# Values of eight tiles projected ahead of the key combine in an attention and ternary feed-forward layer

## The reference

```
h = ln(x)
q = softmax((h Wq^T + bq) Wfq^T + bfq) over all 1024 features; k likewise with Wk, Wfk
v = h Wv^T + bv
per head (16 heads of 64): scores = q k^T; probs = scores / rowsum(scores); ctx = probs v
x = x + ctx
u = ln(x); x = x + bitlinear(silu(bitlinear(u, w_gate)) * bitlinear(u, w_up), w_down)
bitlinear: activations rounded to 127 steps of the row maximum, weights to -1, 0, 1 times their mean magnitude
```

## Time and profile before

| | |
|---|---|
| time, median of 3 runs | 1144.21 us (1143.06 to 1147.94) |
| the profiled execution's own time | 1148.11 us |
| its span on core 4, the slowest | 1146.6 us |
| spans of the other cores | 1123.3 to 1136.8 us |
| TensorE busy, core 4 | 1080.8 us (94%) |
| ScalarE, VectorE, GpSimd busy | 43%, 55%, 18% |
| moved by DMA | 199.66 MB, mean 174 GB/s |

### The profile page before, as it was taken

How to read it: one execution, slowest core, us unless ns; L and a number is a source line. 1 busy time by engine, 2 the same in 40 slices (tenths; PEclk the granted TensorE clock), 3 DMA queues, 4 the chain that set the end, 5 groups by cost and what they waited for, 6 DMA issues and landing times.

```text
span 1146.6 us, 13483 instructions; the slowest of 8 cores (1123.3 to 1146.6 us)
## 1 busy us (share of the span) xinstructions
PE 1080.8 (94%) x5379; PEld 503.7 (44%) x5414; DVE 632.1 (55%) x1140; ACT 491.1 (43%) x604; POOL 204.4 (18%) x132
## 2 busy tenths in 40 slices
PE   5859999999999999897879999999999999999998
PEld 2324454554444544342334444444444444444443
DVE  3356555667766667774826636645645645744311
ACT  2326776677787757564533123223223222222110
POOL 0000000023333330453322012012012012011010
PEclk9979899999998999998989999999999999999999
DMA  8969998689999977779971441441342351231240
GB/s 271 290 198 339 338 334 294 244 276 325 316 325 324 326 222 220 183 215 191 170 132 37 111 96 42 101 108 40 92 105 52 83 120 37 74 92 37 56 110 38
DMA packets 201263, 199.66 MB, mean 174 GB/s; under 512 B 170096, under 2 KB 170096, under 8 KB 193008
## 3 DMA queue, kind: packets, MB, share of 16 engines
q1 hardware_dynamic: 179392, 174.68, 54.2%
q10 hardware_dynamic: 21808, 24.12, 7.5%
HBM read 148.45 MB, written 29.36 MB: 155 GB/s over the span
## 4 chain that ended last, share of the span: by engine, by line
PE 79%; DMA 10%; DVE 4%; ACT 3%; POOL 2%; issue 1%; SPq 1%; ACTq 0%; DVEq 0%
PE ps L563 32%; PE ps L415 25%; PE ps L543 19%; DMA wst<-wdT 4%; DMA stage<-wfkT 2%; DMA wst<-wgT 2%; DMA bvb<-bv 2%; PE ps L464 1%; PE ps L453 1%; SPq L233 1%; ACT wd L348 1%; POOL hmid L1186 1%; POOL wst L326 1%; DVE hmid L1013 1%; DMA xr<-x_oth 1%
## 5 line engine op out<-in xcount | busy, mean ns | idle before, releaser
L563 PE MATMUL ps<-wg,aqT 128*128 128x512 fp8e4 x1024 | 244.9, 382 | 8.6 <-ACT silu L1136 6.0
L563 PE MATMUL ps<-wu,aqT 128*128 128x512 fp8e4 x1024 | 243.2, 381 | 4.1 <-DVE hmid L1013 4.1
L1136 ACT ACTIVATE silu<-ps,l 128x512 f32<-128x512 f32 x128 | 87.7, 686 | 319.5 <-PE ps L563 302.4
L1013 DVE SCALAR_TENSOR_TENSOR hmid<-ps,l,silu 128x512 f32<-128x512 f32 x128 | 95.7, 748 | 146.4 <-PE ps L563 102.2
L326 POOL TENSOR_SCALAR wst<-wst,msum 128x2048 f32<-128x2048 f32 x48 | 95.9, 2001 | 398.6 <-DMA wst<-wgT 292.5
L563 PEld LDWEIGHTS ps<-wu,aqT 128*128 128x128 bf16 x1024 | 100.2, 98 | 127.3 <-DVE hmid L1013 6.3
L563 PEld LDWEIGHTS ps<-wg,aqT 128*128 128x128 bf16 x1024 | 98.8, 99 | 122.4 <-ACT silu L1136 7.1
L415 PE MATMUL ps<-wck,xT 128*128 128x512 bf16 x509 | 127.8, 408 | 13.8 <-DVE xT L745 11.3
L1186 POOL TENSOR_SCALAR hmid<-hmid,hsc 128x1024 f32<-128x1024 f32 x64 | 70.4, 1118 | 306.2 <-DVE hsc L1034 306.2
L415 PE MATMUL ps<-wv,xT 128*128 128x512 bf16 x484 | 116.2, 392 | 5.7 <-ACT ek L1068 3.9
L1005 DVE SCALAR_TENSOR_TENSOR xr<-ps,hsc,xr 128x512 f32<-128x512 f32 x32 | 24.0, 751 | 168.3 <-PE ps L543 168.3
(11 more groups left out here) (95 smaller groups left out, 1064.6 us busy)
## 6 DMA issues: line engine op xcount, KB each, us to landing
wst<-wgT SPq DMA_DIRECT2D x32, 1024.0 KB, 10.6
wst<-wuT SPq DMA_DIRECT2D x32, 1024.0 KB, 9.0
wst<-wdT ACTq DMA_DIRECT2D x19, 1024.0 KB, 7.0
xr<-x_own SPq DMA_DIRECT2D x32, 512.0 KB, 6.9
s_hq<-hqs SPq DMA_DIRECT2D x32, 512.0 KB, 4.1
wst<-wdT SPq DMA_DIRECT2D x13, 1024.0 KB, 8.9
xr<-x_oth SPq DMA_DIRECT2D x16, 512.0 KB, 12.1
y<-xr SPq DMA_DIRECT2D x16, 512.0 KB, 3.4
```

Source lines behind the costliest of these rows:

```text
L563: pe(lambda e, c=c: e.matmul(out, a[:, c * 128:c * 128 + 128], w8[:, c * DI + 512 * oc:c * DI + 512 * oc + 512], start=(c == 0), stop=(c = ...
L1013: dv(lambda e: e.scalar_tensor_tensor(hmid[:, 512 * oc:512 * oc + 512], U[oc % 2], l2[:, s + 6:s + 7], sl, op0=ALU.mult, op1=ALU.mult), [a ...
L1136: ac(lambda e: e.activation(silu[:, (oc % 2) * 512:(oc % 2) * 512 + 512], G[oc % 2], ACTF.Silu, bias=0.0, scale=l2[:, s + 5:s + 6]), [at(" ...
```

## The change

Before slot 0, the values of tiles 0 to 7 come first and the key combine after them.

- Loads: x 0 and 1, then the wvT chunks among x 2 and 3, x 4 to 7, then wfkT in whole rows, then wk in eight blocks of 512 rows by 256 columns (1 KB pieces), bfk, then the first eight of wq and wfqT. bfq and bv come in slot 2. Each bias has its own semaphore, and `BKe` waits for bfk alone.
- TensorE: values of tiles 0 to 3 chunk by chunk in all eight banks (`pe_v4`, in an order sorted by written arrival times), after their transposes in the same banks (`pe_xt4`). Values of tiles 4 to 7 as items, each after the transposes of the next tile. Then eight items `CK` m, each a row block of wck, which waits for all of wfkT and the two wk blocks of column group m div 2; `BK`; `pe_k(0)`; `pe_k(1)`.
- The eight value tiles stay raw in f32 (`vraw`): four in the place of `wcq`, four in the first two `wst` buffers. `ac_ve` reads them there. Hence the query combine's copies wait for `VE`, `cq_slot` is one slot later (5 to 13), and the units of slots 3 to 7 alternate between the last two `wst` buffers (`NB` is 8).
- The units are spread by a nominal slot length (`slot_len`) over slots 3 to 29: 1, 1, 2, 2, 2 in slots 3 to 7, then 3, 4, 3, 3, 3, 3, 3, 2, then in slots 16 to 29 3, 3, 3, 4, 3, 3, 3, 3, 4, 3, 3, 2, 2, 3, and none in 30 and 31.
- `xT` has eight places at first, since tiles 0 to 7 wait there for their key items.

```diff
+    chunks += [rows("wvT", j, wv) for j in range(CH)]
+    chunks += [rows("wfkT", j, wfT) for j in range(CH)]
+    chunks += [block(b, h) for b in range(4) for h in range(2)]
     for j in range(CH):
-        chunks += [("wk", j, 0, D, wnat), ("wfkT", j, 0, 512, wfT)]
...
-        chunks += [("wq", j, 0, D, wnat), ("wfqT", j, 0, D, wfT)]
+        chunks += [rows("wq", j, wnat), rows("wfqT", j, wfT)]
...
     def on_dve(n):
-        return n % 2 == 0
+        return n >= 8 and (n % 2 == 0 if n < NV else n % 4 != 3)
...
+    def pe_v4(i, j):
+        for h in range(2):
+            pe(lambda e, h=h: e.matmul(
+                ps[:, 1024 * i + 512 * h:1024 * i + 512 * h + 512],
+                xT_of(i)[:, j * 128:j * 128 + 128],
+                wv[:, j * D + 512 * h:j * D + 512 * h + 512],
+                start=(j == 0), stop=(j == CH - 1)),
+               [at("XTe", i), cast_of("wvT", j)] if h == 0 else (),
+               ("V", i) if h == 1 and j == CH - 1 else None)
...
-    pe_xt(0)
+    pe_xt(4)
+    for i in range(4, NE):
+        if i + 1 < NE:
+            pe_xt(i + 1)
+        pe_v(i)
+    for m in range(CH):
+        item(("CK", m), lambda c, m=m: wnat[:, c * D + m * 128:
+                                            c * D + m * 128 + 128],
+             w_rhs(wfT), [cast_of("wfkT", 7), cast_of("wfkT", 6),
+                          cast_of("wk", 2 * (m // 2)),
+                          cast_of("wk", 2 * (m // 2) + 1)],
+             ("CK", m), at("CKe", m))
+    item("BK", brep_lhs(0), w_rhs(wfT), [at("brep", 0)], ("BK",), at("BKe"))
     pe_k(0)
-    pe_xt(1)
     pe_k(1)
     for i in range(TKV):
-        pe_v(i)
+        if i >= NE:
+            pe_v(i)
...
     for i in range(TKV):
-        if i < 4:
-            for n in range(NV + 4 * i, NV + 4 * i + 4):
+        if i < 2:
+            for n in range(NV + 8 + 4 * i, NV + 12 + 4 * i):
                 load_chunk(n)
-        if i + 4 < TKV:
+        if i == 2:
+            load_bias("bfq", bqc, ("bfq",))
+            load_bias("bv", bvb, ("biases",))
+        if 4 <= i < TKV - 4:
             load_x(i + 4)
...
+    def v_raw(i):
+        b = (ps[:, 1024 * i:1024 * i + 1024] if i < 4 else
+             AB[item_bank[("V", i)]])
+        evac("v" if i == 2 else "a", vraw(i), b, [at("V", i)], ("VR", i))
...
+    for i in range(5, NE):
+        dv_in(i)
+        dv_xte(i)
+        cast_chunk(2 * i - 2)
+        cast_chunk(2 * i - 1)
+        v_raw(i - 1)
```

More of the change, by code:

```diff
@@ L30 @@
 DEFER = 5
+NE = 8
 NWST = 4
@@ L301, in build_nc @@
     unit_id = {k: n for n, k in enumerate(units)}
-    wslot_of = [n % NWST if n < NA else (n - NA) % NWF
-                for n in range(len(units))]
+    cq_slot = {5 + m: m for m in range(9)}
+    slot_len = [4 + (4 if i >= NE else 0) +
+                (4 if i in cq_slot or TQ <= i < TKV - DEFER else 0)
+                for i in range(TKV - 2)]
+    slot_units = {i: [] for i in range(TKV)}
+    for n in range(NA):
+        want = sum(slot_len[:3]) + (n + 1) * sum(slot_len[3:]) / NA
+        slot_units[next(i for i in range(TKV - 2) if sum(
+            slot_len[:i + 1]) >= want - 1e-6)].append(n)
+    unit_slot = {n: i for i, l in slot_units.items() for n in l}
+    NB = len([n for n in range(NA) if unit_slot[n] < NE])
+    wslot_of = [2 + n % 2 if n < NB else (n - NB) % NWST if n < NA else
+                (n - NA) % NWF for n in range(len(units))]
     before = {}
@@ L306, in build_nc @@
         earlier = [m for m in range(n) if wslot_of[m] == s]
-        before[n] = at("unit", earlier[-1]) if earlier else None
+        before[n] = (at("unit", earlier[-1]) if earlier else
+                     at("VE", 2 * s + 5) if s < 2 else None)
     last_x = max(m for m in range(len(units)) if wslot_of[m] == NWST - 1)
@@ L417, in item @@
                     start=(c == 0), stop=(c == CH - 1)),
-                   (list(after) + [bank_free[b], also_free[b]])
+                   (list(after) + [bank_free[b]])
                    if h == 0 and c == 0 else (),
@@ L426, in x_lhs, with bank4, pe_xt4 @@
     def x_lhs(i):
[L427 to L442, removed]
+        x = xT_of(i)
+        return lambda c: x[:, c * 128:c * 128 + 128]
+    def bank4(i):
+        return ps[:, 1024 * i:1024 * i + 512].bitcast(BF16)
+    def pe_xt4(i):
+        for c in range(CH):
+            pe(lambda e, c=c: e.transpose(
+                bank4(i)[:, c * 128:(c + 1) * 128],
+                xh[:, c * 128:(c + 1) * 128], identb[...]),
+               [at("XH", i), at("ids")] if c == 0 else (),
+               ("XT", i) if c == CH - 1 else None)
+    def pe_v4(i, j):
[7 more added lines that the diff above has]
+               ("V", i) if h == 1 and j == CH - 1 else None)
+    x_in = [9.9, 12.9, 16.3, 21.1]
+    w_in_at = [9.8, 11.4, 14.6, 16.2, 19.4, 21.0, 22.6, 24.2]
+    order4 = [(x_in[i] - 1.4, i, -1) for i in range(4)]
+    order4 += [(max(x_in[i], w_in_at[j]), i, j) for i in range(4)
+               for j in range(CH)]
+    for _, i, j in sorted(order4):
+        if j < 0:
+            pe_xt4(i)
+        else:
+            pe_v4(i, j)
     def brep_lhs(k):
         return lambda c: brep[:, k * D + c * 128:k * D + c * 128 + 128]
-    item("BK", brep_lhs(0), w_rhs(wfT), [at("brep", 0)], ("BK",), at("BKe"))
-    t_free = [at("CKe", 4, 1)]
+    t_free = [at("VR", 2)]
     def pe_xt(i):
```

194 lines of the change are left out of this document (104 added, 90 removed).

## The result

The kernel became slower: 1183.12 us (median of 3 runs, 1182.06 to 1185.04) against 1144.21 of the kernel before in the same comparison. The ratio is 1.0335, with an interval of 1.0292 to 1.0377. The forecast was 1144, the range ended at 1153.

The account below looks back on a forecast made before the run. Phase 1 on core 4 bound by matmuls and 74 weight units, almost together; loads gain 8.3 us, the tail gives back 8.6: +0.3 on 1148.1, less 3.9, 1144.5, said as 1144. Own range 1137 to 1150; with rivals 1130 to 1153.

Parts of the forecast that it names:

- The early stage, step by step: Walk from the first loads through values and key combine to chunk 32, put at 95.3 us.
- pays for the late start: Phase 1 loads: old DMA room at 180 to 260, some 16 us, covers the 12 us late start and leaves 4.
- First matmul near 11: Start of the kernel: TensorE's first matmul was to come near 11 us.
- The last eight matmuls ... 26.6: Values of tiles 0 to 3: after the last wvT chunk's cast, eight matmuls of 1.7 us end them at 26.6.
- Tiles 4 to 7 then go at VectorE's pace ... 4.8: Values of tiles 4 to 7: a VectorE round of 4.8 us against 3.9 for TensorE, V 7 ending at 50.8.
- Combine to chunk 32: Before slot 0: combine starts at 54, eleven items take 38 us to 92, chunk 32 leaves at 95.3.
- Rival C: Early stage: half-clock matmuls make BK late, units go out at 103 instead of 95, time 1152; chance 0.18.
- Rival D: Early loads: x 5 to 7 wait for `xh` of tiles 1 to 3, making wfkT late; 1150 to 1155, chance 0.05.
- K-only slots: Slots 0 to 3, only a K each: 6.0 us a slot, `pe_kv(4)` at about 120.
- From 97 on ... 303: Phase 1 loads after 97: 45.1 and 54.3 MB at 337 and 322 GB/s, 303 us, last unit landing at 399.5.
- The tail: End of phase 1: from unit 73 to the last `pe_kv` 14.2 us, before 5.6, giving back 8.6.
- the 9% of the prediction's line: wk loads: 1 KB pieces 9% slower by a straight line through time per piece, 1.1 us on 4.2 MB, hidden by slack.

Follow-up runs that it names:

- ids_first: Changed kernel with the small identity that the first transposes wait for loaded second instead of tenth; 1173.58 us, ratio 1.0277.
- ids_r_ahead: ids_first plus the next tile's statistics and inverse deviation ordered ahead of the raw copy of the value item before; 1168.07 us, ratio 1.0208.
- gap_two: Changed kernel with units 0 and 1 and x 8 to 11 loaded ahead of chunk 32, the units' sums behind the combine's copies; 1167.3 us, ratio 1.0237.
- before_light: Kernel before with each of the 74 phase 1 units loading a quarter of its columns (other quantized weights and output); 1128.41 us, one run.
- units_to_31: Changed kernel with its units spread over slots 3 to 31 instead of 3 to 29; 1173.75 us, ratio 1.028.
- before_spread: Kernel before with only the changed kernel's number of units in each slot; 1147.14 us, ratio 1.005.
- best: Changed kernel with ids_r_ahead, units_to_31 and gap_two joined, and chunks 24 to 26 cast ahead of the first key logits; 1166.9 us, ratio 1.0199.
- all_four: Changed kernel with ids_r_ahead, units_to_31 and gap_filled joined; 1171.98 us, ratio 1.0305.
- before_bias: Kernel before with only the changed kernel's bias loads and semaphores; 1140.41 us, ratio 0.9989.
- gap_filled: Changed kernel with eight units and x 8 to 11 loaded ahead of chunk 32, the units' sums between the combine's copies on ScalarE; 1169.52 us, ratio 1.0246.
- after_light: Changed kernel with each of the 74 phase 1 units loading a quarter of its columns (other quantized weights and output); 1157.63 us, one run.

## Why the prediction was wrong, step by step

The mechanism was the one described: `BK` holds chunk 32, chunk 32 holds every later load, the transfers rest, and they then run at a full share to the end of phase 1. The failed steps are the sizes of "The early stage, step by step" (chunk 32 at 95.3 was 119.57), the landing of the last unit 15 us later behind that than costed, and the sentence that the old room "pays for the late start".

1. *The begin.* "First matmul near 11" was 19.18: +8. The walk counted the x tiles and the wvT chunks in the queue and left out the identity among them, a load 12.73 from issue to landing. Measured by ids_first: 8.8 at chunk 32 in the median, 6.6 of the time.
2. *"The last eight matmuls ... 26.6".* The values of tiles 0 to 3 ended at 44.0, of which 8 are point 1. The written order puts the transposes of tile 3 late, and 34 of the 64 matmuls stand behind them: 7.50, not 1.7. Even in ids_first they end at 36.2. Nor was this part bound by its loads, as the walk had it: on core 5 of ids_first ScalarE's casts waited for a transfer once (1.19), while the transposes of the four tiles begin at 11.32, 16.88, 22.12 and 28.21, since a tile's statistics stand on VectorE behind the copy of the tile before. That is 5.6 us a tile, a round the walk had only for tiles 4 to 7. No run took this step away.
3. *"Tiles 4 to 7 then go at VectorE's pace ... 4.8".* From the transposes of tile 4 to those of tile 7 it was 21.9, not 13.7. The walk held VectorE's chain but not ScalarE's order, in which the inverse deviation stands behind a copy that waits for the value item. ids_r_ahead measures it: 7.1 at chunk 32 in the median, 7.9 of the time. With it the stage from the end of V 3 to the combine is 25.6 on core 5 (34.9 to 60.5), against 27.4 in the walk, so what is left late at chunk 32 is point 2. In the changed kernel there is also the lower clock: transposes of 1.04 instead of 0.61, V 4 at 5.98 and V 5 at 4.81 instead of 3.62. I had put 1 us down for it, on V 4 alone, and it fell at each thin place (0.81 granted at 40 to 50, 0.67 at 50 to 60).
4. *Combine to chunk 32.* From 77.81 eleven items end at 115.96, 38.2 against 38, and chunk 32 leaves 3.6 later, against 3.3. Correct. So 119.57 against 95.3 is all of points 1 to 3. Rival C had the right sign and the right switch (chunk 32 after 103), and that was in part luck: its mechanism was the half clock, while two orders, of a load and of ScalarE, took 15.9 of the 24. Rival D's wait came as it said (24.31 in the queue for x 4 to 7, since `xh` of tiles 1 to 3 was late), but no engine waited for wfkT: its first cast, on ScalarE at 49.93, had no idle time before it.
5. *K-only slots.* From `pe_kv(0)` to `pe_kv(3)` it was 5.6 a slot, costed at 6.0. But `pe_kv(4)` came 13.4 after `pe_kv(3)` on core 3 (10.2 in the median): unit 0's load stood behind ten transfers released at once, and ScalarE, whose next entry it was, waited 7.18 for it ahead of the exponentials of tile 4. With light loads this slot is 8.2. This wait was in no term.
6. *"From 97 on ... 303".* The bytes and rates were right for the long stretches: 99.7 MB between 125 and 440, at 333 and 320 GB/s, against 337 and 322. What wasn't is the start of it: 64 GB/s at 110 to 125, since chunks 32 to 39 are paced by their casts, and 281 at 125 to 180, since with two `wst` buffers unit 2 waits until 149.0 for the end of unit 0. The last unit was 39.3 late against 399.5 (438.81), 24.3 of it from chunk 32. The others, some 15, are mostly these two stretches (55 us x (337 - 281)/337 is 9).
7. *"The old room pays for the late start."* The rest of the transfers was worth keeping: gap_two gains 11.2 us by a use of it. I had made the loads the only clock of phase 1, and what binds is a chain of both; before_light shows that even the kernel before had its FF 13.0 (cores 0 to 3) to 15.4 (all) later with its full loads.
8. *The tail.* From the last unit's multiplication to the last `pe_kv` it was 15.7, forecast 14.2, and from there 18.66 to the feed-forward part, as before. Right. But the spreading costs in slots 15 to 26 too, where four units are more than ScalarE and the loads get through in a slot: units_to_31 is worth 6.3 of the time and 6.7 of FF, before_spread 6.8 of FF.

By the ratio the slowdown is 38 us, against none forecast. 14.5 of it are points 1 and 3 by their runs. Chunk 32 is still 7.7 late in ids_r_ahead in the median, 7 at the same 0.92 (an estimate), which is point 2. units_to_31 gives 6.3. The last 10 are the other waits of points 5 to 7, which no run separates; gap_two, which moves all of them at once, is worth as much. The terms overlap and each has several us of noise, so the sum is rough. That best has its FF within 3.3 us of the kernel before (4.3 on cores 0 to 3) says that the list is nearly whole up to the feed-forward part. It says as well that the reordering, freed of these, gains nothing there.

The cites of the Trainium skill (DMA: Bandwidth & Descriptors, Specifications) decided little. About 358 GB/s for a core was not seen in any long stretch here; 343 in best is the nearest. On the 1 KB pieces the trace does decide: from 56 to 72 the changed kernel moved hardly anything but wk blocks, 17.9 to 20.8 GB/s for each busy engine over the eight cores, median 20.2, where the long stretches gave 20.8 (333 in 16 engines). That is 3% slower and not the 9% of the prediction's line, nearer to the page's rule of full rate from 512 B.

*Not settled:* why two cores of a die run at 0.81 for over 100 us in best and all_four; what two `wst` buffers instead of four in slots 3 to 7, a price of the raw values, cost by themselves, since no run has the one without the other; how much of the light runs is clock; and what takes back before_bias's gain at FF.

## What to carry to other kernels

When a stage is moved to the front, walk every in-order queue for it, ScalarE's and the load queue's too: a small constant issued tenth and a copy that stands ahead of two 0.3 us activations were worth some 14.5 of the 38 us. If one item late in that stage releases the rest of a load queue, its lateness goes on nearly one for one (0.92 at the first feed-forward matmul here), so price a mistake there as such, and put loads that have their own buffers ahead of the blocked entry, with their consumers behind whatever the stage waits for. A full DMA share does not say that bytes are the only limit: quarter the bytes in both kernels before building on it, and look at the clock of every core before calling the difference a wait.

## What the runs showed of the hardware

- In best, cores 4 and 5 were granted 0.81 of the clock from 120 to 240 while core 0 of the same program had 1.00, and FF came over 20 us later on them than on the six others. In all_four it was cores 6 and 7, with 0.71 on core 7 at 80 to 100. It came in every run of these two kernels, on changing pairs, and in few of the others (one of before_bias's twelve, one of gap_filled's four, and on four cores one of after_light's two). The lowest mean clock of a core of the kernel before is 0.969; these pairs have 0.960 to 0.962.
- In the profiled execution of the kernel before, cores 4 to 7 ran at 0.92 to 0.93 from 260 to 400 and cores 0 to 3 at 0.99 to 1.00, at 317 to 324 GB/s on all eight. With the loads cut to some 140 GB/s all eight had 1.00 in before_light and in after_light. The loads alone don't tell the two dies apart.
- 1 KB pieces moved at 20.2 GB/s for each busy engine, large ones at 20.8 (changed kernel: median over the cores at 56 to 72, and core 3 at 180 to 260).
- A 32 KB load behind eight of 0.5 MiB landed 12.73 us after its issue; issued second, in ids_first, it took 3.3.
